# The experts' silu in a scan kernel: tanh, biases added by TensorE, two wide VectorE products

## What is computed

```python
# one direction of the state-space block
carry = dA_t * carry + dBu_t            # over 512 positions, 16 states, 512 channels
y_t = einsum('bdn,bn->bd', carry, C_t)
# the experts (x_MD: the tokens, n: the expert)
h = einsum('md,ndh->nmh', x_MD, Wl1) + bl1[:, None, :]
a, b = h[..., :512], h[..., 512:]
y = einsum('nmh,nhd->nmd', silu(a) * b, Wl2) + bl2[:, None, :]
```

## Time and profile before

| | us |
|---|---|
| median of 3 runs | 3296.14 (3295.69 to 3296.49) |
| the profiled execution, its own time | 3288.68 |
| its span, first to last instruction | 3286.9 |
| one batch of the hardware loop (1186.7 to 1439.2) | 252.5 |
| of it: TensorE busy | 211.4 |
| VectorE busy | 228.2 |
| ScalarE busy | 182.3 |
| GpSimd busy | 203.6 |

### The profile page before, as it was taken

One profiled execution on the slowest core, in us unless ns is written; L12 is line 12 of the kernel. 1 busy time (PEld: TensorE's weight loads), 2 busy tenths in 40 slices (PEclk: granted clock), 3 DMA queues, 4 the chain that ended last, 5 costly groups with the idle time before them and its releaser, 6 DMA issues. The chain is left out here.

```text
span 3286.9 us, 40509 instructions
## 1 busy us (share of the span) xinstructions
PE 2753.8 (84%) x13518; PEld 1831.7 (56%) x13518; DVE 2251.9 (69%) x2812; ACT 1766.4 (54%) x2690; POOL 1756.1 (53%) x555
## 2 busy tenths in 40 slices
PE   5466798887887887887888888656999999999999
PEld 4234565565665565665565566544455555555564
DVE  5278989989989989989989989954432442442430
ACT  1355767767767757858848758521331332322322
POOL 0699868868868868878878878741000000000000
PEclk9777898898898998989999989787999999999999
DMA  6212333323334333323333333322000000000000
GB/s 251 94 67 98 124 110 110 136 94 127 112 106 139 107 111 132 115 98 119 129 101 125 107 105 138 107 94 89 26 32 0 32 32 0 32 28 4 6 7 7
DMA packets 149279, 283.24 MB, mean 86 GB/s; under 512 B 23660, under 2 KB 97879, under 8 KB 149079
## 3 DMA queue, kind: packets, MB, share of 16 engines
q1 hardware_dynamic: 142934, 264.08, 23.6%
q0 software_dynamic: 6144, 16.79, 1.5%
HBM read 239.13 MB, written 41.68 MB: 85 GB/s over the span
## 5 line engine op out<-in xcount | busy, mean ns | idle before, releaser
L620 POOL TENSOR_TENSOR hs<-u,bb 128x2048 f32<-128x2048 f32 x256 | 1159.4, 4535 | 360.3 <-PE hT L908 330.1
L789 DVE TENSOR_TENSOR_SCAN hs<-dA,hs 128x1024 f32<-128x1024 f32 x512 | 1165.5, 2282 | 123.4 <-POOL hs L620 72.9
L706 ACT ACTIVATE dA<-dt,cols 128x511 f32<-128x511 f32 x1024 | 661.8, 680 | 420.3 <-DVE hs L789 416.0
L908 PE MATMUL hT<-ident,hs 128*128 128x128 f32 x3584 | 558.0, 297 | 271.0 <-DVE held L799 226.6
L908 PEld LDWEIGHTS hT<-ident,hs 128*128 128x128 f32 x3584 | 434.0, 151 | 413.9 <-DVE held L799 299.7
L799 DVE SCALAR_TENSOR_TENSOR held<-hT,ct,held 128x512 f32<-128x512 f32 x864 | 602.5, 740 | 50.2 <-PE hT L908 49.5
L1210 ACT ACTIVATE gl<-bank,cols_sb 128x512 f32<-128x512 f32 x192 | 130.4, 686 | 534.9 <-PE bank L1462 534.6
L1118 POOL COPY cur<-slot 128x8 uint32 (+1 forms) x8 | 1.5, 187 | 704.3 <-DVE xh L1260 664.4
L1462 PE MATMUL bank<-mT,cms_sb 128*128 128x512 f32 x768 | 362.7, 597 | 10.1 <-ACT mT L1204 8.6
L927 PE MATMUL moe<-xgT,held 128*128 128x128 f32 x2400 | 335.6, 300 | 32.6 <-ACT xgT L720 31.4
L927 PEld LDWEIGHTS moe<-xgT,held 128*128 128x128 f32 x2400 | 323.0, 215 | 64.0 <-ACT xgT L720 41.0
(11 more groups left out here) (220 smaller groups left out, 3425.9 us busy)
## 6 DMA issues: line engine op xcount, KB each, us to landing
held<-wl SPq DMA_DIRECT2D x75, 1024.0 KB
bb<-b_scratch SPq DMA_DIRECT2D x128, 512.0 KB
held<-wl SPq DMA_DIRECT2D x75, 512.0 KB
xg_scratch<-zero SPq DMA_DIRECT2D x10, 960.0 KB, 5.3
xg<-xg_scratch SPq DMA_DIRECT2D x75, 128.0 KB
yg_scratch<-yg SPq DMA_DIRECT2D x75, 128.0 KB, 1.7
cb<-b_scratch SPq DMA_DIRECT2D x32, 256.0 KB
cms_sb<-cms SPq DMA_DIRECT2D x2, 3072.0 KB, 16.6
```

The lines of the kernel that those rows point to most:

```text
L620: nc.gpsimd.tensor_tensor(hs[n % HS][:, :, :], u[d][:, :, :], row, ALU.mult).then_inc(dBu_ready, 1)
L706: last = nc.scalar.activation(dst, src, ACT.Exp, scale=cols[:, at:at + 1])
L789: nc.vector.tensor_tensor_scan(h, decay, h, 0.0, ALU.mult, ALU.add).then_inc(scan_done, 1)
L908: last = nc.tensor.transpose(hT[c % 2][:, k * P:(k + 1) * P], hs[n % HS][:, k, c * P:(c + 1) * P], ident[:, :])
```

## The change

The silu is written as `a * (1 + tanh(a / 2)) / 2`, and the work is divided in another way:

- both biases are added by TensorE: the pieces "a" and "b" each begin with one product of 128x512 over 4 partitions, whose moving operand `sel` (4 x 512) picks for each block of 128 columns the bias row that belongs to it; the 8 block matmuls then add to it;
- ScalarE does one tanh of 128x512 in place of four silus of 128x128, with no bias;
- VectorE gets a new piece "half" in the slot that was empty, `(tanh + 1) * a`, and "gate" becomes `0.5 * b` times that: one instruction of 128x512 each, both read `moe`. They stand behind the slot's weighing, where the gate stood ahead of it;
- "b" on TensorE waits for "half" (`a_used`), where it waited for the silu (`sa_ready`): VectorE still reads `a` in `moe`;
- in the first block the bias table is loaded, transposed by one TensorE instruction, copied by ScalarE and stored to `b1_dram`; each tile then loads its two rows of biases from there as 4 x 2 x 128 in place of 128 x 8;
- `one_row` becomes a slice of `sel`, for which GpSimd does a memset and an affine_select, and TensorE waits for both.

```diff
@@ the first block, SyncE, ScalarE, TensorE @@
+                sp.dma_start(b1_cols[:, :, :], bl1c.rearrange("e p m -> p e m")).then_inc(b1_in, 16)
...
+                sp.wait_ge(b1_ready, 1)
+                sp.dma_start(b1_dram.rearrange("e g m p -> (e g m) p"), b1_rows[:, :]).then_inc(b1_out, 16)
...
+                sp.wait_ge(b1_out, 16)
...
+                act.wait_ge(b1_ps, 1)
+                nc.scalar.activation(b1_rows[:, :], bankR[4][0:NE * 2 * HB, 0:P], ACT.Copy).then_inc(b1_ready, 1)
...
+                pe.wait_ge(b1_in, 16)
+                nc.tensor.transpose(bankR[4][0:NE * 2 * HB, 0:P], b1_cols[:, :, :].rearrange("p e m -> p (e m)"), ident[:, :]).then_inc(b1_ps, 1)
...
@@ the second block: pieces, loads, setup @@
-                    for at, piece in enumerate(("x", "a", "", "b", "gate", "down")):
+                    for at, piece in enumerate(("x", "a", "half", "b", "gate", "down")):
...
-                    sp.dma_start(b1[r][:, :], bl1c[e]).then_inc(e_in[r], 16)
+                    sp.dma_start(b1[r][:, :, :], b1_dram[e].rearrange("g m p -> m g p")).then_inc(e_in[r], 16)
...
-                nc.gpsimd.memset(one_row[:, :], 1.0).then_inc(setup_g, 1)
+                nc.gpsimd.memset(sel[:, :, :], 1.0).then_inc(setup_g, 1)
+                pool.wait_ge(setup_g, 1)
+                nc.gpsimd.affine_select(out=sel[:, :, :], in_=sel[:, :, :], compare_op=ALU.is_equal, fill=0.0, base=0,
+                                        pattern=[[-1, HB], [0, P]], channel_multiplier=1).then_inc(setup_g, 1)
...
@@ ScalarE @@
-                        for m in range(HB):
-                            last = nc.scalar.activation(sa[:, m, :], moe[:, m * P:(m + 1) * P], ACT.Silu, bias=b1[r][:, m:m + 1])
-                        last.then_inc(sa_ready, 1)
+                        nc.scalar.activation(sa[:, :, :], moe[:, :].rearrange("p (m t) -> p m t", t=P), ACT.Tanh, scale=0.5).then_inc(sa_ready, 1)
...
@@ VectorE @@
-                    dve.wait_ge(sa_ready, t + 1)
-                    dve.wait_ge(b_ps, t + 1)
-                    for m in range(HB):
-                        last = nc.vector.scalar_tensor_tensor(out=sa[:, m, :], in0=moe[:, m * P:(m + 1) * P],
-                                                              scalar=b1[r][:, HB + m:HB + m + 1], in1=sa[:, m, :],
-                                                              op0=ALU.add, op1=ALU.mult)
-                    last.then_inc(hE_ready, 1)
+                    if piece == "half":
+                        dve.wait_ge(sa_ready, t + 1)
+                        nc.vector.scalar_tensor_tensor(out=sa[:, :, :], in0=sa[:, :, :], scalar=1.0, in1=ab,
+                                                       op0=ALU.add, op1=ALU.mult).then_inc(a_used, 1)
+                    elif piece == "gate":
+                        dve.wait_ge(b_ps, t + 1)
+                        dve.wait_ge(a_used, t + 1)
+                        nc.vector.scalar_tensor_tensor(out=sa[:, :, :], in0=ab, scalar=0.5, in1=sa[:, :, :],
+                                                       op0=ALU.mult, op1=ALU.mult).then_inc(hE_ready, 1)
...
-                                for piece, i in tiles[2 * n + j]:
-                                    if piece == "gate":
-                                        gate(b, i)
...
+                                for piece, i in tiles[2 * n + j]:
+                                    expert(piece, b, i)
...
@@ TensorE @@
-                            pe.wait_ge(sa_ready, t + 1)
+                            pe.wait_ge(a_used, t + 1)
                         at = 0 if piece == "a" else HB
+                        mm(moe[:, :], b1[r][:, at // HB, :], sel[:, :, :].rearrange("k m t -> k (m t)"), start=True, stop=False,
+                           skip_group_check=True)
                         for m in range(HB):
                             for k in range(KD):
                                 last = mm(moe[:, m * P:(m + 1) * P], w1[r][:, k, (at + m) * P:(at + m + 1) * P], xgT[:, k, :],
-                                          start=(k == 0), stop=(k == KD - 1))
+                                          start=False, stop=(k == KD - 1), skip_group_check=True)
```

More of the change, by code:

```diff
@@ L85, in bass_mamba_moe_then_linear_attention_mlp @@
     s_dram = scratch("s_scratch", (NB, P, NC, DM))
+    b1_dram = scratch("b1_scratch", (NE, 2, HB, P))
     x_v = x.rearrange("b (c p) d -> b p c d", p=P)
@@ L140, in bass_mamba_moe_then_linear_attention_mlp @@
             w_r = sr("w_r", [P, KD, NE])
+            b1_cols = sr("b1_cols", [P, NE, 2 * HB])
+            b1_rows = sr("b1_rows", [NE * 2 * HB, P])
             rows = sr("rows", [P, 2, NE])
@@ L165, in bass_mamba_moe_then_linear_attention_mlp @@
             aT_outs = [sem("aT_out0"), sem("aT_out1")]
+            b1_in, b1_ps, b1_ready, b1_out = (sem(n) for n in ("b1_in", "b1_ps", "b1_ready", "b1_out"))
             bankR = [ps(f"rbank{i}", [P, 512], layR) for i in range(8)]
@@ L351, in bass_mamba_moe_then_linear_attention_mlp @@
         with lay0:
-            one_row = s0("one_row", [1, P])
             xnT = s0("xnT", [P, KD, L])
@@ L368, in bass_mamba_moe_then_linear_attention_mlp @@
             w2 = [part(RING * N_W1 + i * N_W2, N_W2, DM) for i in range(RING)]
-            b1 = [s0(f"b1_{i}", [P, 2 * HB]) for i in range(RING)]
+            b1 = [s0(f"b1_{i}", [HB, 2, P]) for i in range(RING)]
+            sel = s0("sel", [HB, HB, P])
             b2 = [s0(f"b2_{i}", [1, DM]) for i in range(RING)]
@@ L393, in bass_mamba_moe_then_linear_attention_mlp @@
             y_st = [sem(f"yg_stored{i}") for i in range(RING)]
-            xgT_ps, xgT_ready, a_ps, b_ps, sa_ready, hE_ready, l2_ps, yg_ready = (
-                sem(n) for n in ("xgT_ps", "xgT_ready", "a_ps", "b_ps", "sa_ready", "hE_ready", "l2_ps", "yg_ready"))
+            xgT_ps, xgT_ready, a_ps, a_used, b_ps, sa_ready, hE_ready, l2_ps, yg_ready = (
+                sem(n) for n in ("xgT_ps", "xgT_ready", "a_ps", "a_used", "b_ps", "sa_ready", "hE_ready", "l2_ps", "yg_ready"))
             POOLN = (2, 9)
@@ L801, in weigh, with expert @@
                     ins.then_inc(hT_used, 1)
-                def gate(b, i):
-                    t, r = TPB * b + i, i % RING
-                    dve.wait_ge(sa_ready, t + 1)
-                    dve.wait_ge(b_ps, t + 1)
-                    for m in range(HB):
-                        last = nc.vector.scalar_tensor_tensor(out=sa[:, m, :], in0=moe[:, m * P:(m + 1) * P],
-                                                              scalar=b1[r][:, HB + m:HB + m + 1], in1=sa[:, m, :],
-                                                              op0=ALU.add, op1=ALU.mult)
-                    last.then_inc(hE_ready, 1)
+                def expert(piece, b, i):
+                    t = TPB * b + i
+                    ab = moe[:, :].rearrange("p (m t) -> p m t", t=P)
+                    if piece == "half":
[7 more added lines that the diff above has]
+                                                       op0=ALU.mult, op1=ALU.mult).then_inc(hE_ready, 1)
                 def finish(b, k):
@@ L854, in _ @@
                 pe.wait_ge(w_sem, 16 * N_W)
-                pe.wait_ge(setup_g, 1)
+                pe.wait_ge(setup_g, 2)
                 def prepare(what, k, d, unit, b, first=False):
@@ L933, in tile @@
                             mm(moe[:, 0:DM], sa[:, m, :], w2[r][:, m, :], start=(m == 0), stop=False)
-                        mm(moe[:, 0:DM], one_row[:, :], b2[r][:, :], start=False, stop=True).then_inc(l2_ps, 1)
+                        mm(moe[:, 0:DM], sel[0:1, 0, :], b2[r][:, :], start=False, stop=True).then_inc(l2_ps, 1)
                 def body(b, last_batch):
```

## The result

The changed kernel takes 3397.42 us (median of 4 runs, 3394.59 to 3404.95), the one before, measured beside it, 3295.91 (3294.54 to 3296.49). The ratio (changed over before) is 1.0308, with a 95% interval of 1.0293 to 1.0324: about 101 us slower. The prediction said 3392 us and 3320 to 3418. So the two traces differ by 116 us where the medians differ by 101, and about an eighth of what the traces show is the choice of execution.

The account below looks back on a forecast made before the run. TensorE never pauses in two stretches, only 0.4 us ahead of VectorE; odd units 51, last 4 and even units 43 add 98 us to 3288.7: 3387, or 3394 on the median's scale. Predicted 3392 us, range 3320 to 3418.

Parts of the forecast that it names:

- What bounds the kernel: Scan stage: TensorE never pauses in slots 0 to 9 (even unit) and 0 to 15 (odd), 0.4 us ahead of VectorE.
- ScalarE's part: One tanh replaces silus and table loads: ScalarE relieved of 210 us, only 6 us on the path, in even units.
- VectorE's part: Two wide instructions take 1.32 us, four narrow gates 1.01: 0.3 us more per tile, 23 us over 75 tiles.
- TensorE's part: Two added bias products of 128x512 over 4 partitions in each tile, 150 in all, priced at 1.05 us each.
- 0.17 us more: One-row product of 256 columns costs 0.62 us, a 128-row one 0.455; the 0.17 was added to 0.86.
- The half-clock price: Tile 3's "a" in each unit: its bias product at half clock costs about 2.0 us.
- The even unit's path: Tile 0's "down" delays ScalarE's copy, the last `xc` and GpSimd: VectorE's 3.83 us wait for GpSimd grows by 2.1.
- The sum: Whole kernel: 7 odd units x 7.3, the last 4, 7 even units x 6.2, together 98 us more.
- Hidden: TensorE's fullness is slack that VectorE doesn't feel; only VectorE's 23 us less 6 stay: 3313 us, chance 0.13.
- half hidden: Even unit absorbs its share in GpSimd's and ScalarE's waits, or full clock lasts longer: 3335 to 3365 us, chance 0.07.
- The new wait at "half": VectorE stands at "half" until the tanh is done, 0.3 us in each of 75 tiles: 3417 us, chance 0.1.
- Faster: ScalarE's relief reaches VectorE through waits for decays and turns: at most 39 us less, 3257 us, chance 0.06.

## Why the prediction was right, point by point

**What bounds the kernel: right.** TensorE was full in the stretches named, with 0.4 us of lead. Products added there are paid nearly in full: those of tiles 0 to 2, five of them ahead of slot 14's turn, gave 5.5 us in the odd unit, where 5 x 1.26 less the lead is 5.9.

**ScalarE's part: right in size and place.** Forecast was 210 us less ScalarE and 6 us less time; the stage of the scans has 214.4 less, and the tanh alone measured 4.9 us. This line of the groups

```profile
L723 ACT ACT_TABLE_LOAD x63 | 80.8, 1283 | 2.5 <-issue 1.4
```

holds the decays' own switches, and no line has one for the tanh. The odd unit's wait stands at 3.82 us as before. One detail was wrong: the even unit's 0.87 vanishes with the tanh alone, but in the changed kernel 0.34 of it is left, with the products and without them. And a new wait for a decay came up in the odd unit, by which 1.2 us of TensorE's lateness reach VectorE,

```profile
1429.21 2.29 DVE L804 TENSOR_TENSOR_SCAN hs<-dA,hs 128x1024 f32<-128x1024 f32 x1 [1.21 <-ACT dA L723]
```

while one for GpSimd in the kernel before is gone:

```profile
1338.99 2.29 DVE L789 TENSOR_TENSOR_SCAN hs<-dA,hs 128x1024 f32<-128x1024 f32 x1 [0.80 <-POOL hs L620]
```

The two do not stand in one place: the wait for GpSimd came five scans earlier in the unit. The run without products still has it, and has none for that decay, so both are effects of the products:

```profile
1342.15 2.29 DVE L804 TENSOR_TENSOR_SCAN hs<-dA,hs 128x1024 f32<-128x1024 f32 x1 [0.99 <-POOL hs L637]
```

In the changed kernel, ahead of that decay ScalarE does the silu of `xc` with its two table loads, and first waits for the convolution's last result from the full TensorE:

```profile
1422.65 0.69 ACT L684 ACTIVATE xc<-prep,cols 128x512 f32<-128x512 f32 x1 [2.84 <-PE prep L899]
```

**VectorE's part: over-sized.** The term was 0.31 us a tile, 23 us, from the price of two weighings (0.66 each). The new instructions cost 0.59 each and the term is 0.17 a tile; busy time without the products rose by 10.5 us. The weighing, of the same shape, was near but not near enough. And the small waits that I counted as gone, under 1 us in each unit, and the tanh's 0.6 us in the even one were enough to hide all that was left: a unit without products is as long as before (131.2 for 131.1, 121.3 for 121.5).

**TensorE's part: the mis-sized term.** The working took 1.05 us from a range of 0.86 to 1.2. The product costs 1.26, just outside the upper end: 1.05 behind its own start, but 0.10 ahead and 0.11 behind, too. The step that failed is "0.17 us more": it compared start to start of the one-row product alone and left out that the products ahead of it already took 1.82 for 1.73. With the way back named but not taken into the middle value, the error was 0.21 us on 150 products. The half-clock price (2.0) was right.

**The even unit's path: partly wrong.** The prediction led the first 2.1 us through "down", the last `xc` and GpSimd into VectorE's wait for GpSimd. That wait did not grow, 3.84 us for 3.83. VectorE had by then lost the time to two new waits for the turn, 1.28 and 0.92; this is also one reason why the waits for the turn rose by more than was forecast. The amount by the end of tile 2 was nearly right all the same (4.2 for 3.6), so the place was wrong and the amount about right.

**The sum: right, in part by luck.** In the traces the odd unit lost 7.4 us (forecast 7.3), the even one 8.0 (6.2), the batch 15.7 (13.5); the two traces are 15 us further apart than the medians, so these are the upper side. The products' own terms, 7 x 6.85 and 7 x 6.65 and some 3.5 for the last unit, are 98 us. Taken away from the changed kernel they measured 107 (1.0308 less 0.9982), and the rest, 0 by the same working, 6 us of gain: two errors of opposite sign. Put into the kernel before they measured 96, and the rest 6 us of loss on top. Either way the total, 98 forecast and 101 measured, agrees better than the parts do, and that the two differ by only 3 us is luck. By place, with tiles 0 to 2 or 3 and 4 alone: the five products of the odd stretch and the four of the even one were too cheap by 0.6 each time, the odd unit's slow one too dear by 0.4.

**Rivals.** Hidden (3313) and half hidden are out: the waits for the turn rose by 95 us, where some 60 had been forecast. The new wait at "half" isn't there. Faster: its mechanism exists, at 5 us and not 39. The Trainium skill (ScalarE: Activation LUTs, Table sets: the hidden batching unit) has tanh in one set with exp, and the trace agrees: the loads are missing. But the gain was off the path. What the Trainium skill says of height, that a product over 32 rows takes as long as one over 128 (TensorE: Matmul & The Clock Gate, Why this matters for your kernels), doesn't carry over to fewer rows here, in a stream of 128-row products: 1.26 us for 4 rows, 0.86 for 128. No run had one of 32 rows.

## What to carry to other kernels

Before work is moved to another engine, find the stretches in which that engine never pauses and read its lead over the one that takes its results; past that lead most of what is added is paid (here 4.2 us of 5.0 and 5.5 of 6.3), however much is saved on an engine that is waited for only here and there. Price a small odd-shaped product by its neighbours, too: the time of the row ahead and that of the row behind belong to it, as far as they are longer with it than without. A bias product of one or four rows between 128-row products was better padded with zeros to 128 rows, in both kernels, and better still left to the engine that adds it in an instruction it issues anyway.

## What the runs showed of the hardware

A product with few rows costs more than a full one. Between f32 products over 128 rows, one of 128x512 over 4 rows costs 1.26 us and over 128 rows 0.86; one of 256 columns over one row costs 0.28 us more than over 128, its row ahead included (2.44 for 2.16). About 0.1 us of each falls on the row ahead, and of the wide one as much on the row behind; behind the narrow one the turn takes 0.93 us for 0.87. Widening took 39 us off the changed kernel for two products a tile, 8 more for the third, and 9 to 10 off the kernel before for that one; in the first case the granted clock rose as well (0.93 for 0.922 to 0.924), and part of the 39 us is that; in the last it was 0.918 for 0.913, and its part is open. The Trainium skill (TensorEngine Tiling (Array Packing), Key Properties) says that a change of the tiling mode drains TensorE; time lost at both edges of the product would fit that, but no run here tests whether a mode is what changes.

A VectorE instruction of 128x512 with one operand in PSUM cost 0.59 us as half or gate and 0.66 as a weighing; no run looked for the reason.
